# Four moves at the first batches of three stages, and the last batch's schedule a step forward

## The chip, the cores and the metric

The kernel runs on one core of a Trainium2 chip. The metric is the device time of one execution in microseconds. The engines are TensorE (PE in the rows, its weight loads PEld), VectorE (DVE), ScalarE (ACT), GpSimd (POOL) and SyncE (SP, which issues most DMAs).

## The reference, cut to what matters

Four layers, each on x of 8 batches of 256 tokens by 512 features: an attention over the context, an attention over channels, a transformer layer (two attentions over tokens and a gelu MLP), and a recurrent block. In all but the first two the change has a place:

```
# tokens: q, k, v of the normalised rows; then
x = x + gelu(layernorm(x) @ w1 + b1) @ w2 + b2
# recurrent block
xa = ln(x); sx = previous_token(xa) - xa
xxx = tanh((xa + sx * maa_x) @ maa_w1) ...
r, k, v, g = projections of the five mixtures xm
s = k_t v_t + w_t * s;  out_t = r_t (u * k_t v_t + s)      # the scan over tokens
x1 = x + groupnorm(out) * silu(g) @ Wo.T
xc = ln(x1); sx2 = previous_token(xc) - xc
out = x1 + sigmoid((xc + sx2 * fr) @ Wfr.T) * (square(relu((xc + sx2 * fk) @ Wfk.T)) @ Wfv.T)
```

## The kernel before, in words

Five stages follow one another with a barrier between them: `context_attention`, `channel_attention`, `token_attentions`, `token_mlp`, `recurrent_block`. `Ahead` holds the tiles and `AheadSignals` the semaphores that live across a barrier, so that a stage loads rows and weights for the next one. Each stage has one instruction list per engine, and engines meet by semaphores only; all queues are in order. Semaphores of a ring get a credit first, by `open_loop` on SP (line 38), one instruction for each; an engine that waits on such a semaphore also waits for this.

`token_attentions` splits each fp32 operand in a rounded high part (ScalarE) and a low part (VectorE's subtraction), and a projection is three products of parts. Batch 0's projections are the units Q0, Q1, K0, K1, V0, V1 on TensorE (`fill`, lines 1618 and 1620). SP loads the V weights of the first layer in `before` (line 1460), into two tiles of the probabilities; ScalarE's `before` (from line 1813) keeps Q0, Q1, K0, K1, then rounds V (`round_first_values`, line 1755), and VectorE splits it (line 1915).

`token_mlp` runs 8 steps a batch. In step n TensorE does the hidden unit n (24 matmuls, line 2288), now and then the transposes of the next batch's normalised rows (`turn`, line 2275), and the output unit n - 3 (12 matmuls, line 2303). ScalarE evicts a hidden unit with its square (lines 2342, 2345), does the tanh of the one before (`bend`) and rounds it (`round_hidden`, line 2356). VectorE multiplies (line 2471) and finishes the gelu (`gelu`, line 2463), GpSimd multiplies for the cube (line 2257) and takes the low part (line 2226). During batch 0, twelve halves of weights (`HALVES`) are also rounded by ScalarE (`round_half`, line 2334) and split by VectorE (`split_half`, line 2429); `SPLIT_BY` gives how many by which step: 2, 4, 6, 8, 9, 10, 11, 12. They pass through three staging tiles, and SP reloads one when its half is split. `rows_step(b)` says in which step batch b + 1's statistics are taken; normalising follows a step later, and `turn_half` puts its two groups of transposes 2 and 4 steps behind, with VectorE's split one step after each:

```
for k in halves_in(b, n):
    split_half(k)
if b + 1 < BATCH:
    if n == rows_step(b):       statistics(b + 1); moment(b + 1)
    elif n == rows_step(b) + 1: normalise(b + 1)
    elif turn_half(b, n - 1) is not None: split_turned(...)
```

`recurrent_block` pipelines three batches. Batch b's 16 scans (`step`: VectorE's product, line 3420, and scan, line 3423; GpSimd's product, line 2912; TensorE's spread and sum, lines 3050 and 3061) run along with the units of the batch ahead (A: norm, transposes T, difference SX, low-rank XX, mixtures M, K, V, R, G and C) and of the batch behind them, Z: E, Q, N, O, then LS and LN (norm of x1), T, X (difference and mixes), FK, FR, FV. Tables such as `LAST_SCHEDULE` write out by hand which units stand in which of the 16 steps. A unit in a table costs an engine its own part only; each waits on semaphores for the rest. The first batch has a `PROLOGUE` without scans, in which `keep_busy` issues 52 transposes on TensorE whose result nobody reads (the filler), ahead of XX0 (line 2969). `finish` does the last batch's tail after its last scan.

## Time and profile before

| | us |
|---|---|
| median of 3 runs (3635.02 to 3637.12) | 3635.35 |
| the profiled execution | 3639.3 |
| its span, first to last instruction | 3637.5 |
| TensorE busy | 3411.6 (94%) |
| VectorE busy | 2321.6 (64%) |
| GpSimd busy | 2022.3 (56%) |
| ScalarE busy | 1821.5 (50%) |

A row of the order of time has the start, the duration (of the whole group if it has more than one instruction), the engine, the line, the operation, output and inputs, their shapes and the count; in brackets stands how long the engine was idle before it and what released it. `issue` there means that the profile shows no releaser. Times are microseconds from the span's start.

### The profile page before, as it was taken

The numbers are of one execution on the slowest core, as the hardware profiler recorded it, in microseconds if no ns is written. First come the engines' busy times: TensorE is split into PE (matmuls) and PEld (weight loads), VectorE is DVE, ScalarE is ACT, GpSimd is POOL, SyncE is SP. The second block draws the span as 40 slices with busy tenths as digits, with TensorE's granted clock in tenths as the row PEclk, the third lists the DMA queues.
The fourth block names the chain that finished last, engine by engine and source line by source line (L and its number), as shares of the span: only waits on it lengthen the run. The fifth ranks groups of instructions, "written<-read, shape, count | busy, mean of one in ns | idle before, by whom it ended". The sixth has DMA issues, their size and how long they took to land. (4 is left out here: it accounts for less than half of the span.)

```text
span 3637.5 us, 59766 instructions
## 1 busy us (share of the span) xinstructions
PE 3411.6 (94%) x23502; PEld 2613.9 (72%) x23502; DVE 2321.6 (64%) x2874; ACT 1821.5 (50%) x4228; POOL 2022.3 (56%) x1103
## 2 busy tenths in 40 slices
PE   8989999999999999979999999699998899999978
PEld 6878778877887787657887788599985555555544
DVE  2455565566556656748777877665545678877776
ACT  2134664565456546656776776555543334343322
POOL 2235664575557556625665666455544566767753
PEclk9999999999999999989999999899998899999989
DMA  4331111121112111120002111210003000000000
GB/s 133 109 131 47 68 67 56 59 72 62 48 68 72 60 47 47 59 99 24 31 30 82 53 42 49 92 38 24 24 24 126 13 8 11 18 19 18 13 18 12
DMA packets 114302, 188.80 MB, mean 52 GB/s; under 512 B 18416, under 2 KB 36848, under 8 KB 113520
## 3 DMA queue, kind: packets, MB, share of 16 engines
q1 hardware_dynamic: 111856, 180.89, 14.8%
q8 instruction: 183, 3.00, 0.3%
q10 hardware_dynamic: 2176, 4.19, 0.3%
q14 instruction: 87, 0.71, 0.1%
HBM read 159.89 MB, written 25.17 MB: 51 GB/s over the span
## 5 line engine op out<-in xcount | busy, mean ns | idle before, releaser
L1030 POOL TENSOR_TENSOR l_pr<-l_pr,l_inv 128x1024 f32<-128x1024 f32 x256 | 479.7, 1894 | 383.1 <-DVE l_inv L1092 383.1
L900 ACT ACTIVATE l_pr<-l_ps_s,l_top 128x512 f32<-128x512 f32 x512 | 348.0, 689 | 352.7 <-DVE l_top L1088 275.9
L1547 POOL TENSOR_TENSOR tok_pr<-tok_pr,tok_ma 128x1024 f32<-128x1024 f32 x128 | 305.8, 2411 | 268.5 <-DVE tok_pr L1932 268.5
L2912 POOL TENSOR_TENSOR rec_rs<-rec_sE,rec_rT 128x1024 f32<-128x1024 f32 x128 | 316.7, 2474 | 231.6 <-DVE rec_sE L3423 183.3
L1025 POOL TENSOR_TENSOR l_x_lo<-ahead_piece,l_x_hi 128x1024 fp32r<-128x1024 f32 (+1 forms) x97 | 294.0, 3031 | 154.2 <-ACT l_x_hi L884 154.2
L1088 DVE TENSOR_REDUCE l_top<-l_ps_s 128x2 f32<-128x1024 f32 x256 | 304.1, 1218 | 10.5 <-PE l_ps_s L674 10.4
L3423 DVE TENSOR_TENSOR_SCAN rec_sE<-rec_wE,rec_ps_v 128x1024 f32<-128x1024 f32 x128 | 292.7, 2286 | 4.4
L684 PE MATMUL l_ps_t<-l_ident,l_pr 128*128 128x128 f32 x2048 | 275.7, 278 | 10.5 <-POOL l_pr L1030 4.5
L684 PEld LDWEIGHTS l_ps_t<-l_ident,l_pr 128*128 128x128 f32 x2048 | 225.9, 141 | 77.7 <-issue 60.7
L1807 ACT ACTIVATE tok_pr<-tok_pr,tok_shift 128x256 f32<-128x256 f32 x512 | 253.3, 497 | 10.2 <-DVE tok_shift L1940 9.6
L635 PE MATMUL l_ps_b<-l_x_hi,l_w_lo 128*128 128x256 f32 x784 | 226.7, 289 | 0.0
L635 PE MATMUL l_ps_b<-l_x_hi,l_w_hi 128*128 128x256 f32 x784 | 221.2, 282 | 0.0
L635 PE MATMUL l_ps_b<-l_x_lo,l_w_hi 128*128 128x256 f32 x784 | 221.1, 282 | 0.0
L1940 DVE TENSOR_REDUCE tok_shift<-tok_pr 128x4 f32<-128x1024 f32 x128 | 155.6, 1216 | 48.9 <-POOL tok_pr L1547 48.6
L3420 DVE TENSOR_TENSOR rec_ps_v<-rec_ps_v,rec_kT 128x1024 f32<-128x1024 f32 x128 | 156.5, 1223 | 37.7 <-ACT rec_kT L3274 27.6
L1096 DVE COPY l_pT<-l_ps_t 128x512 f32<-128x512 f32 x256 | 174.3, 681 | 2.9 <-PE l_ps_t L684 2.6
L905 ACT ACTIVATE l_pT<-l_ps_t 128x512 f32<-128x512 f32 x256 | 152.3, 595 | 22.9 <-PE l_ps_t L684 22.8
L1932 DVE TENSOR_TENSOR tok_pr<-tok_ps_s,tok_mk 128x1024 f32<-128x1024 f32 x128 | 155.7, 1217 | 7.4 <-PE tok_ps_s L1630 7.4
L1641 PE MATMUL tok_ps_t<-tok_ident,tok_pr 128*128 128x128 f32 x1024 | 139.1, 280 | 17.5 <-DVE tok_pT L1945 11.1
L1116 DVE TENSOR_TENSOR l_o_lo<-l_ps_a,l_o_hi 128x512 fp32r<-128x512 f32 x64 | 44.2, 691 | 170.0 <-ACT l_o_hi L910 170.0
L662 PE MATMUL l_ps_b<-l_wv_lo,l_x_hi 128*128 128x256 f32 x512 | 149.4, 292 | 1.9 <-DVE l_v_later L1102 0.8
L635 PEld LDWEIGHTS l_ps_b<-l_x_hi,l_w_lo 128*128 128x128 f32 x784 | 148.2, 189 | 2.8 <-issue 1.0
(519 smaller groups left out, 9701.0 us busy)
## 6 DMA issues: line engine op xcount, KB each, us to landing
ahead_piece<-x SPq DMA_DIRECT2D x63, 512.0 KB, 3.9
ahead_piece<-in_c SPq DMA_DIRECT2D x63, 512.0 KB, 4.8
ahead_rows<-x SPq DMA_DIRECT2D x22, 512.0 KB, 3.8
ahead_piece<-in_L_w_qk SPq DMA_DIRECT2D x16, 512.0 KB, 6.0
x<-tok_xb SPq DMA_DIRECT2D x16, 512.0 KB, 2.8
l_xt<-in_xT SPq DMA_DIRECT2D x8, 512.0 KB, 6.3
l_ct<-in_cT SPq DMA_DIRECT2D x8, 512.0 KB, 7.2
l_xn<-in_x SPq DMA_DIRECT2D x8, 512.0 KB, 4.7
```

Of the source, the lines that this page charges most:

```text
L635: mm = pe.matmul(bank[:, here], w[:, part, half * SLOTS + s, :], x[b % 2][:, s, here], start=(s == 0 and w is w_lo), stop=(s == SLOTS - 1 ...
L684: mm = pe.transpose(ps_t[h][:, m, :], pr[t][:, h, m * P:(m + 1) * P], ident[:, :])
L900: act.activation(pr[t][:, h, :], ps_s[:, t % 2, h, :], ACT.Exp, bias=top[:, t, h:h + 1], accum_out=mass[:, t, h:h + 1]).then_inc(exped, 1)
L1025: pool.tensor_tensor(x_lo[b % 2][:, which, :], rows, x_hi[b % 2][:, which, :].bitcast(F32), ALU.subtract).then_inc(x_split, 2 if source is ...
L1030: pool.tensor_tensor(pr[t][:, :, :], pr[t][:, :, :], inv[:, t, :].unsqueeze(2).to_broadcast([P, 2, FEAT]), ALU.mult).then_inc(scaled, 1)
L1088: dve.tensor_reduce(top[:, t, :], ps_s[:, t % 2, :, :], AXIS.X, ALU.max, negate=True).then_inc(topped, 1)
L1096: dve.tensor_copy(pT[1][:, :, t * P:(t + 1) * P], ps_t[1][:, :, :]).then_inc(turned_kept[1], 1)
L1547: pool.tensor_tensor(tile, tile, ma[u][:, :, :].rearrange("p t k -> p (t k)").unsqueeze(1).to_broadcast([P, 2, TT * TOK]), ALU.add).then_i ...
L1807: ins = act.activation(tile, tile, ACT.Exp, bias=shift[n % RING][:, i, m:m + 1], accum_out=mass[n // 2 % 2][:, m, n % 2 * 2 + i:n % 2 * 2 ...
L2912: pool.tensor_tensor(rs[j % 2][:, :, :], sE[j % 2][:, :, :], rT[s][:, :, :], ALU.mult).then_inc(rs_made, 1)
L3420: dve.tensor_tensor(ps_v[j % 2][:, :, :], ps_v[j % 2][:, :, :], kT[s][:, :, 0:TOK], ALU.mult).then_inc(kv_made, 1)
L3423: dve.tensor_tensor_scan(sE[j % 2][:, :, :].rearrange("p c t -> p (c t)"), wE[s][:, :, :].rearrange("p c t -> p (c t)"), ps_v[j % 2][:, :, ...
```

## The change

It has five places.

- `token_attentions`: the two loads of the first V weights stand at the head of SP's list, ahead of the credits; ScalarE rounds them after Q1 is kept, ahead of K0.
- `token_mlp`: `rows_step(0)` returns 2, not 1; ScalarE's `round_hidden` stands ahead of `round_half` in a step; SP loads the recurrent block's columns and first edge after the last half. (The staging tiles get a name for their number; it stays 3.)
- `recurrent_block`, first batch: columns and edge are there already; `maa_w1` is loaded ahead of the credits; the edge is copied ahead of T0; VectorE, not GpSimd, takes the difference, in two halves behind T0 and T1; the filler has 30 transposes; the first states are loaded later in SP's list.
- `FIRST_TENSOR_SCHEDULE`: G0 ahead of C in step 1.
- `LAST_SCHEDULE`: LN joins LS in step 8, and all Z units behind it stand one step earlier; VectorE's X too.

```diff
@@ -63,6 +63,9 @@
     def __init__(self, nc, rows_ctx, ctx):
...
+        self.cols = rows_ctx.enter_context(nc.sbuf_tensor("ahead_cols", [P, 16, FT], F32))
+        self.edge = rows_ctx.enter_context(nc.sbuf_tensor("ahead_edge", [P, FT, 2], F32))
         self.rows = rows_ctx.enter_context(nc.sbuf_tensor("ahead_rows", [P, TT, FEAT], F32))
@@ -1413,6 +1416,9 @@
         def _(sp):
+            for k in range(2):
+                source = layers[0].w["QKVO".index("V")][2 * k * P:2 * (k + 1) * P, :].rearrange("(t p) n -> p t n", p=P)
+                sp.dma_start(first_v(k), source).then_inc(first_v_loaded, 16)
             open_loop(sp, loop_sems)
@@ -1455,9 +1461,6 @@
                     sp.dma_start(qk_sb[i][:, :, :], layers[i].qk).then_inc(small_loaded, 16)
-                for k in range(2):
-                    source = layers[0].w["QKVO".index("V")][2 * k * P:2 * (k + 1) * P, :].rearrange("(t p) n -> p t n", p=P)
-                    sp.dma_start(first_v(k), source).then_inc(first_v_loaded, 16)
                 load_x(1, 1, 0)
@@ -1823,9 +1826,11 @@
                 act.wait_ge(bias_scaled, len(layers))
-                for unit in UNITS[:4]:
+                for unit in UNITS[:2]:
                     keep(1, 0, unit, 0)
                 round_first_values()
+                for unit in UNITS[2:4]:
+                    keep(1, 0, unit, 0)
                 normalise(1, 1)
@@ -2090,7 +2096,7 @@
-        return 1 if b == 0 else 0
+        return 2 if b == 0 else 0
@@ -2207,6 +2213,9 @@
                 load_half(k)
+            next_cols, next_state = recurrent
+            sp.dma_start(ahead.cols[:, :, :], next_cols).then_inc(following.piece_loaded[0], 16)
+            sp.dma_start(ahead.edge[:, :, :], next_state[0:1, :, :, :].rearrange("o p t n -> p (o t) n")[:, :, 0:2]).then_inc(following.piece_loaded[1], 16)
             sp.wait_ge(here.last_stored, 16)
@@ -2375,10 +2384,10 @@
                     bend(*before(b, n, 1))
+                if b or n:
+                    round_hidden(*before(b, n, 1))
                 for k in halves_in(b, n):
                     round_half(k)
-                if b or n:
-                    round_hidden(*before(b, n, 1))
                 if turn_half(b, n) is not None:
@@ -2513,7 +2522,7 @@
     FIRST_TENSOR_SCHEDULE = (
-        "L:R1 A:T0 A:T1", "L:C L:G0", "A:XX0 A:XX1", "L:G1", "A:Mwk0", "A:Mwk1", "A:Mvr0 A:Mvr1", "A:D1", "A:K0",
+        "L:R1 A:T0 A:T1", "L:G0 L:C", "A:XX0 A:XX1", "L:G1", "A:Mwk0", "A:Mwk1", "A:Mvr0 A:Mvr1", "A:D1", "A:K0",
         "A:K1 A:Mgd0", "A:R0 A:Mgd1", "A:R1", "A:V0", "A:V1 A:C B:T0 B:T1", "A:G0 B:XX0 B:XX1", "A:G1 B:Mwk0 B:Mwk1")
@@ -2540,10 +2549,10 @@
     LAST_SCHEDULE = (
-        "", "Z:E", "Z:Q Z:I", "Z:N1", "Z:N2", "Z:N3", "Z:O0", "Z:O1", "Z:LS", "Z:LN", "Z:T0 Z:T1 Z:X", "Z:XA Z:XR",
-        "Z:FK0", "Z:FK1", "Z:FR0", "Z:FR1")
+        "", "Z:E", "Z:Q Z:I", "Z:N1", "Z:N2", "Z:N3", "Z:O0", "Z:O1", "Z:LS Z:LN", "Z:T0 Z:T1 Z:X", "Z:XA Z:XR", "Z:FK0",
+        "Z:FK1", "Z:FR0", "Z:FR1", "")
     LAST_VECTOR_SCHEDULE = (
-        "", "Z:E", "", "Z:I", "", "Z:N3", "", "", "Z:LS", "", "", "Z:X", "", "", "", "")
+        "", "Z:E", "", "Z:I", "", "Z:N3", "", "", "Z:LS", "", "Z:X", "", "", "", "", "")
     SUB, HALF = 4, P // 2
@@ -2626,8 +2634,8 @@
         w_loaded, ident_made, const_made, power_made = sem("w_loaded"), sem("ident_made"), sem("const_made"), sem("power_made")
-        a_edge_loaded = sem("a_edge_loaded")
-        cols_loaded, x_loaded, st_loaded, z_loaded, stored = sem("cols_loaded"), here.rows_loaded, [sem(f"st_loaded{u}") for u in range(2)], sem("z_loaded"), sem("stored", 16)
+        a_edge_loaded, halves_shifted = here.piece_loaded[1], sem("halves_shifted")
+        cols_loaded, x_loaded, st_loaded, z_loaded, stored = here.piece_loaded[0], here.rows_loaded, [sem(f"st_loaded{u}") for u in range(2)], sem("z_loaded"), sem("stored", 16)
         a_filled, z_filled, z_kept = sem("a_filled", NA), sem("z_filled", NZ), sem("z_kept", NZ)
@@ -2759,6 +2767,7 @@
         def _(sp):
+            sp.dma_start(m1[:, :, :], maa_w1.rearrange("(t p) n -> p t n", p=P)).then_inc(m1_loaded, 16)
             open_loop(sp, loop_sems)
@@ -2784,16 +2793,13 @@
-            sp.dma_start(col[:, :, :], cols).then_inc(cols_loaded, 16)
-            load_edge(0)
-            sp.dma_start(m1[:, :, :], maa_w1.rearrange("(t p) n -> p t n", p=P)).then_inc(m1_loaded, 16)
-            load_st(0, 0)
             sp.dma_start(m2[:, :, :], maa_w2).then_inc(w_loaded, 16)
...
             sp.dma_start(mean_of[:, :], group_mean).then_inc(w_loaded, 16)
+            load_st(0, 0)
             for n in "kvrg":
@@ -2859,6 +2865,8 @@
                                        ALU.add).then_inc(mixtures, 1)
+                elif unit == "SX" and b == 0:
+                    pool.wait_ge(mixed_x, of(b, 1, 0))
                 elif unit == "SX":
@@ -2966,7 +2974,7 @@
                 if unit == "XX0" and b == 0:
-                    keep_busy(pe, ps_acc[:, 0, 0:P], ident, 52)
+                    keep_busy(pe, ps_acc[:, 0, 0:P], ident, 30)
                     pe.wait_ge(const_made, CONSTANTS)
@@ -3166,7 +3174,7 @@
                     act.wait_ge(mixtures, of(b - 1, 5, 4))
-                elif unit == "T1":
+                if unit == ("T1" if b else "T0"):
                     act.wait_ge(a_edge_loaded, (b + 1) * 16)
@@ -3335,8 +3343,14 @@
                         dve.wait_ge(cols_loaded, 16)
-                    dve.wait_ge(shifted, of(b, 1, 0))
+                    else:
+                        dve.wait_ge(shifted, of(b, 1, 0))
                     for c in range(FT):
+                        if b == 0 and c % 2 == 0:
+                            dve.wait_ge(keeps(b, f"T{c // 2}"), kept_by(b, f"T{c // 2}"))
+                            dve.tensor_tensor(sx[:, c:c + 2, :], xaT[:, c:c + 2, 0:TOK], xaT[:, c:c + 2, 1:TOK + 1],
+                                              ALU.subtract).then_inc(halves_shifted, 1)
+                            dve.wait_ge(halves_shifted, c // 2 + 1)
                         ins = dve.scalar_tensor_tensor(out=xm[0][:, c, :], in0=sx[:, c, :], scalar=col[:, MAA_X, c:c + 1],
```

## Rows read from the trace of the kernel before

**Rows 1.** By stage: window, busy of each engine (instructions), granted clock, DMA share, GB/s
```profile
1588.00:2334.00 746.00, 699.00 (x6562) 571.25 (x6562) 552.23 (x688) 498.50 (x1427) 424.23 (x255) 0.97 0.15 50
2334.00:2723.00 389.00, 373.56 (x2400) 337.56 (x2400) 210.80 (x230) 203.43 (x430) 204.79 (x156) 0.98 0.12 40
2723.00:3637.00 914.00, 799.65 (x3918) 500.40 (x3918) 667.57 (x581) 304.78 (x689) 558.30 (x304) 0.95 0.08 26
```

**Rows 2.** Order of time at the token attentions: start, duration, instruction, idle before it
```profile
1592.37 0.34 SPq L1456 DMA_DIRECT2D tok_ln_cols<-in_L_ln  x1
...
1596.90 1.91 ACT L1772 ACTIVATE tok_lnT<-tok_ps_t,tok_ln_cols 128x256 f32<-128x256 f32 x4
...
1606.21 0.84 ACT L1747 ACTIVATE tok_qT<-tok_ps_s,tok_qk_cols 128x256 f32<-128x256 f32 x2 [1.84 <-PE tok_ps_s L1620]
...
1611.17 0.63 PE L1620 MATMUL tok_ps_s<-tok_lnT_lo,tok_w_hiK 128*128 128x256 f32 x4
...
1612.57 2.00 ACT L1755 ACTIVATE tok_w_hiV<-tok_pr 128x1024 fp32r<-128x1024 f32 x2
...
1617.06 2.05 PE L1618 MATMUL tok_ps_p<-tok_w_hiV,tok_lnT_hi 128*128 128x512 f32 x4 [5.26 <-issue]
...
1624.47 1.09 PE L1618 MATMUL tok_ps_o<-tok_w_hiV,tok_lnT_lo 128*128 128x512 f32 x4
...
1625.40 1.04 PE L1590 MATMUL tok_ps_t<-tok_ident,ahead_xn 128*128 128x128 f32 x8
```

**Rows 3.** DMAs, 1588 to 1612: count, KB each, median us from issue to landing
```profile
tok_pr<-in_L_xattn_w_qkv SPq DMA_DIRECT2D x2, 512.0 KB, 4.1
...
tok_qk_cols<-in_L_qk SPq DMA_DIRECT2D x2, 4.0 KB, 2.0
```

**Rows 4.** Order of time in the MLP's first batch
```profile
2353.72 1.06 ACT L2334 ACTIVATE mlp_w_hi<-mlp_xb 128x1024 fp32r<-128x1024 f32 x1 [2.52 <-DMA mlp_xb<-in_L_xattn_w]
...
2363.78 1.09 PE L2275 MATMUL mlp_ps_t<-mlp_ident,ahead_xn 128*128 128x128 f32 x4 [10.98 <-DVE ahead_xn L2408]
...
2371.26 0.40 PE L2303 MATMUL mlp_ps_y<-mlp_w_lo,mlp_hid_hi 128*128 128x512 f32 x1
...
2373.59 1.83 DVE L2463 SCALAR_TENSOR_TENSOR ahead_piece<-ahead_piece 128x512 f32<-128x512 f32 x1
...
2383.16 2.41 POOL L2238 TENSOR_TENSOR mlp_xb<-ahead_rows,mlp_b 128x1024 f32<-128x1024 f32 x1
...
2384.65 1.21 DVE L2471 TENSOR_SCALAR ahead_piece<-ahead_piece 128x512 f32<-128x512 f32 x1 [2.61 <-ACT ahead_piece L2345]
...
2391.26 0.28 PE L2288 MATMUL mlp_ps_h<-mlp_ln_hi,mlp_w_lo 128*128 128x256 f32 x1
```

**Rows 5.** Order of time at the recurrent block's start
```profile
2725.05 7.51 PE L59 MATMUL rec_ps_acc<-rec_ident 128*128 128x128 f32 x52
...
2727.51 1.02 ACT L3184 ACTIVATE rec_xaT<-rec_ps_a,rec_cols 128x256 f32<-128x256 f32 x2 [11.55 <-DMA rec_cols<-in_L_cols]
...
2731.83 1.68 DVE L3340 SCALAR_TENSOR_TENSOR rec_xm<-rec_sx,rec_cols,rec_xaT 128x256 f32<-128x256 f32 x4 [7.34 <-POOL rec_sx L2865]
...
2733.65 2.51 PE L2988 MATMUL rec_ps_a<-rec_xm,rec_m 128*128 128x256 f32 x10 [1.10 <-DVE rec_xm L3340]
```

**Rows 6.** Order of time around unit C of batch 0
```profile
2787.95 1.08 PE L2998 MATMUL rec_ps_a<-rec_sx,rec_hs_u 128*32 128x256 f32 x8 [3.48 <-issue]
...
2789.82 5.63 PE L2936 MATMUL rec_ps_a<-rec_xm,rec_w_g 128*128 128x256 f32 x16
...
2792.06 1.67 DVE L3340 SCALAR_TENSOR_TENSOR rec_xm<-rec_sx,rec_cols,rec_xaT 128x256 f32<-128x256 f32 x4 [1.75 <-POOL rec_sx L2865]
```

**Rows 7.** Order of time in the last batch
```profile
3563.11 5.65 DVE L3403 SCALAR_TENSOR_TENSOR rec_xk<-rec_sq,rec_cols,rec_xcT 128x256 f32<-128x256 f32 x4 [0.88 <-POOL rec_sq L2888]
...
3579.84 1.23 DVE L3420 TENSOR_TENSOR rec_ps_v<-rec_ps_v,rec_kT 128x1024 f32<-128x1024 f32 x1 [0.73 <-ACT rec_kT L3274]
...
3589.74 0.69 DVE L3432 TENSOR_TENSOR rec_bonus<-rec_ps_acc,rec_bonus 128x512 f32<-128x512 f32 x1 [6.34 <-PE rec_ps_acc L3061]
```

More of the change, by code:

```diff
@@ L2070, in weight_columns, with token_mlp @@
     return w1[:, i * FEAT:(i + 1) * FEAT].rearrange("(t p) n -> p t n", p=P)
-def token_mlp(nc, semaphores, x, w1_d, w2_d, ln_cols, b1, b2, out, ahead, here, following):
+def token_mlp(nc, semaphores, x, w1_d, w2_d, ln_cols, b1, b2, out, ahead, here, following, recurrent):
     HID = 4 * FEAT
@@ L2080, in token_mlp @@
     HALVES = [(n, i, k) for n, i in (("w2", 0), ("w1", 2), ("w2", 1), ("w1", 3), ("w2", 2), ("w2", 3)) for k in range(2)]
-    LAST_IN_XB = (len(HALVES) - 1) // 3 * 3
+    STAGES = 3
+    LAST_IN_XB = (len(HALVES) - 1) // STAGES * STAGES
     SPLIT_BY = (2, 4, 6, 8, 9, 10, 11, 12)
@@ L2126, in token_mlp @@
         xb = sb("xb", [P, TT, FEAT])[:, :, :]
-        spare = sb("spare", [P, 2, FEAT])
+        spare = [sb(f"spare{i}", [P, 2, FEAT])[:, :, :] for i in range(1)]
         w2_lo = sb("w2_lo", [P, 2 * CHUNKS, FEAT], F32R)
         res = sb("res", [P, TT, FEAT])[:, :, :]
-        stages = (xb, res, spare[:, :, :])
+        stages = (xb, res, *spare)
         ps_h = [ps(f"ps_h{i}", [P, 2, TOK]) for i in range(2)]
@@ L2140, in token_mlp @@
             sem(n) for n in ("norm_loaded", "b1_loaded", "b2_loaded", "ident_made", "const_made"))
-        half_loaded = [sem(f"half_loaded{i}") for i in range(3)]
+        half_loaded = [sem(f"half_loaded{i}") for i in range(STAGES)]
         piece_hi, piece_split, half_hi, half_split = (sem(n) for n in ("piece_hi", "piece_split", "half_hi", "half_split"))
@@ L2193, in load_half @@
                 n, i, half = HALVES[k]
-                if k >= 3:
-                    sp.wait_ge(half_split, k - 2)
+                if k >= STAGES:
+                    sp.wait_ge(half_split, k - STAGES + 1)
                 if n == "w1":
@@ L2199, in load_half @@
                     source = w2_d[(4 * i + 2 * half) * P:(4 * i + 2 * half + 2) * P, :]
-                sp.dma_start(stages[k % 3], source.rearrange("(t p) n -> p t n", p=P)).then_inc(half_loaded[k % 3], 16)
+                sp.dma_start(stages[k % STAGES], source.rearrange("(t p) n -> p t n", p=P)).then_inc(half_loaded[k % STAGES], 16)
             sp.dma_start(ln_sb[:, :, :], ln_cols).then_inc(norm_loaded, 16)
@@ L2332, in round_half @@
             def round_half(k):
-                act.wait_ge(half_loaded[k % 3], 16 * (k // 3 + 1))
-                act.activation(half_of(k, 0), stages[k % 3], ACT.Copy).then_inc(half_hi, 1)
+                act.wait_ge(half_loaded[k % STAGES], 16 * (k // STAGES + 1))
+                act.activation(half_of(k, 0), stages[k % STAGES], ACT.Copy).then_inc(half_hi, 1)
             def evict(b, n):
@@ L2428, in split_half @@
                     dve.wait_ge(here.last_stored, 16)
-                dve.tensor_tensor(half_of(k, 1), stages[k % 3], half_of(k, 0).bitcast(F32), ALU.subtract).then_inc(half_split, 1)
+                dve.tensor_tensor(half_of(k, 1), stages[k % STAGES], half_of(k, 0).bitcast(F32), ALU.subtract).then_inc(half_split, 1)
             def next_statistics():
@@ L2575, in recurrent_block @@
         mean_of = sb("mean_of", [P, P])
-        NC = 16
-        col = sb("cols", [P, NC, FT])
+        col = ahead.cols
         LN1_W, LN1_B, LN2_W, LN2_B, MAA_X, DECAY0, U, GN_W, GN_B, FFN_K, FFN_R, STACK = range(12)
@@ L2586, in recurrent_block @@
         st = [sb(f"st{u}", [P, FT, 2 + GROUP]) for u in range(2)]
-        edge, a_edge = sb("edge", [P, FT, 2]), sb("a_edge", [P, FT, 2])
+        edge, a_edge = sb("edge", [P, FT, 2]), ahead.edge
         xaT, sx = sb("xaT", [P, FT, TOK + 1]), sb("sx", [P, FT, TOK])
@@ L2638, in recurrent_block @@
         shifted, mixed_x, products, mixtures, decayed, g_bent, v_hi_kept = (
-            sem("shifted", 1), sem("mixed_x", 1), sem("products", 5), sem("mixtures", 5), sem("decayed", 1), sem("g_bent", 2), sem("v_hi_kept", 2))
+            sem("shifted", 1, 3), sem("mixed_x", 1), sem("products", 5), sem("mixtures", 5), sem("decayed", 1), sem("g_bent", 2), sem("v_hi_kept", 2))
         spread_v, kv_made, seeded, scanned, rs_made, summed = (
@@ L3530, in build @@
     semaphores.clear(kept)
-    token_mlp(nc, semaphores, x4, ap["L2_xattn_w1"], ap["L2_xattn_w2"], ap["L2_ln3"], ap["L2_b1"], ap["L2_b2"], x5, ahead, for_mlp, for_recurrent)
+    token_mlp(nc, semaphores, x4, ap["L2_xattn_w1"], ap["L2_xattn_w2"], ap["L2_ln3"], ap["L2_b1"], ap["L2_b2"], x5, ahead, for_mlp, for_recurrent,
+              (ap["L3_cols"], ap["L3_state"]))
     early.close()
```

## The prediction

> **What bounds the kernel now.** I read the table of stages first: TensorE is busy for 94% of the token attentions, 96% of the MLP and 87% of the recurrent block [rows 1], so an edit pays only where TensorE stands still, and all edits of this change lie at such places: the first batch of three stages, and the last batch of the last one. Then I read the order of time at each place. In the token attentions TensorE ends the K projections at 1611.8 and starts V at 1617.06 [rows 2]. In the MLP it stands 10.98 us before the transposes of batch 1, because VectorE has not normalised those rows [rows 4]. At the recurrent block's start ScalarE waits for the column constants until 2727.51, and a filler of 52 transposes bridges the time until 2733.65 [rows 5]. In the last batch VectorE needs 5.65 us for four small mixes and at the end waits 6.34 us for the last sum [rows 7].
>
> **1. First V weights (token attentions).** Two edits belong together: SP issues the two V loads ahead of its credits, and ScalarE rounds V behind the second Q unit, not behind the second K unit. Now TensorE's last K matmul ends at 1611.8 (1611.17 + 0.63), ScalarE first keeps that unit, rounds V from 1612.57 for 2.00, VectorE's split takes about 2.4, and TensorE idles 5.26 [rows 2]. After: ScalarE is free at 1607.05 (1606.21 + 0.84), rounds until 1609.1, still ahead of the K0 unit's end at about 1609.0, and VectorE, idle there, has split by 1611.5. TensorE is through K1 at 1611.8 and goes straight on: 5.3 us off the path. The 24 V matmuls took 8.34 us (1617.06 to 1625.40), the first four 2.05, the last four 1.09; with groups of four 0.93 apart, as the last two are (1624.47 to 1625.40), all would take 5.6: the idle had dropped the granted clock to 1.2 GHz. Without it another 2.7 goes. Next late would be the normalised rows of batch 1 (ScalarE 1612.7 to 1614.2) and the mask; both are early. Sum: -8.1. The next short stall, at 1627.5 to 1629.6, stays.
> The loads cost SP two issues of 0.45 us ahead of its credits and ahead of the small loads. The small ones land 2.0 us after issue now [rows 3]; SP issues the first of four at 1592.37 [rows 2], the last 1.4 later, so it would be 1594.7, landed at 1596.7, and ScalarE wants it at 1596.90 [rows 2]: cost 0, up to 0.5 if it lands late. The Trainium skill ("DMA: Bandwidth & Descriptors", Queues, rings and completion order) says that each ring consumes descriptors in order, so the small loads would now queue behind 1 MB of V; an estimate from the 4.1 us to landing puts V's end at 1595, before their own 1596.7, and the sum is the same by either.
>
> **2. The MLP's first batch.** Two edits: rows_step(0) goes from 1 to 2, so that statistics, normalise, transposes and split of batch 1 come a step later (transposes in steps 4 and 6, splits in 5 and 7); and ScalarE rounds the hidden layer (round_hidden) ahead of the weight halves. I wrote out the order of each engine, step by step, with the durations of the rows: a hidden unit 2.7, an output unit 2.8 (TensorE does 7 units and one transpose group from 2371.26 to 2391.26 [rows 4]), eviction 1.43, a rounded half 0.95, a split 1.2, gelu 0.6, GpSimd's products 1.3, a load 4. Two things matter in it. A VectorE operation that meets a GpSimd one waits until that ends: 1.83 for a gelu of 0.68, 1.21 for a multiply of 0.43, while GpSimd's bias addition ran until 2385.57 [rows 4]. And evict 2 stands behind a rounded half whose load lands at 2353.72 [rows 4], in both orders. For the kernel before this schedule gives the transposes at 2363.9 (row: 2363.78) and batch 1's first hidden unit at 2390.2 (row: 2391.26), so I trust it to about 1 us.
> For the changed kernel: output unit 0 is no longer behind the transposes and runs at 2353.8, hidden 4 at 2356.6 to 2359.5. Then TensorE comes to the transposes, in step 4. Their rows are normalised in VectorE's step 3, behind two more halves: gelu 1 ends 2358.4, round_hidden 1 2359.0, halves 4 and 5 are rounded by 2361.0 and split by 2362.7, statistics 2364.1, gelu 2 2365.1, halves 6 and 7 rounded by 2367.7 and split by 2370.35, normalised 2371.3. TensorE waits 11.8, not 10.98, and starts output 1 at 2371.7, now at 2371.26 [rows 4]: **the first wait is moved, not removed**. From there the later splits bite. Batch 1's hidden unit needs the second split of its rows, now in step 7. ScalarE evicts hidden 7 by 2393.0, gelu 6 ends 2395.5 (behind GpSimd's product), round_hidden 6 2396.1, half 11, which the new order puts behind it, 2397.1, its split 2398.6, cast and split of the rows 2399.7. TensorE would be ready at 2391.7: a **new wait of 8 us**. From there the stage has no slack: its TensorE is idle 15.4 us in all [rows 1], mostly the known wait. So 2399.7 less 2391.3 is +8.4; the slow clock behind the first long wait costs 1.2 as it does now (the schedule has full clock, and this is carried into the second chain), and behind the second wait 1.2 more: +10.8. Bounds: +6 if the waits for GpSimd vanish, +13 if both waits cost 2.7 in clock, as in part 1.
> The rows show VectorE's operation blocked for the whole of GpSimd's. The Trainium skill ("SBUF — State Buffer", SBUF: two separate sides) gives that as an exclusive lock of a shared port pair, which speaks against packing gelu and splits between GpSimd's products: schedule against schedule the change loses 9.5 with it (2390.2 to 2399.7) and 5.9 without it. By that rule, the trace agrees.
>
> **3. The recurrent block's start.** Columns and edge are loaded during the MLP, m1 ahead of the credits, the difference of batch 0 moves from GpSimd (1.89) to VectorE in halves, between ScalarE's two evictions, and the filler has 30 transposes. TensorE's transposes start some 0.45 later, since SP's credits stand behind m1's issue. ScalarE evicts at once (2725.3 to 2727.2, now 2727.51 to 2729.66), VectorE subtracts (0.69 twice) and mixes (1.68): done 2729.5, now 2733.51. The filler now needs 7.51 [rows 5]; at the full clock, that the second half of it has, one costs about 0.12 (eight in 1.04 with the last one's drain [rows 2]), so 22 fewer save 2.6 by the clock and 3.2 by the mean. It ends at 2730.7: **-3.0** against 2733.65, and the filler, not the mix, is late last. Bounds -2.5 and -4. The two added DMAs in the MLP hide behind SP's wait for the biased rows; the six narrow weights have 1.9 us left, the wide ones 4.
>
> **4. G0 ahead of C.** TensorE waits 3.48 for GpSimd's product before C [rows 6]. G0 fills that hole, but batch 1's XX0 then waits for its mix (2792.06 + 1.67), so that the hole comes back and the slow clock with it: -0.5, between -2 and +1.
>
> **5. Last batch.** From LN on, each unit of the batch in front comes a step earlier. VectorE's mix X (5.65 of which 4 are waiting for GpSimd [rows 7]) then comes before scan 11 instead of behind it: step 12 starts at 3569.6 to 3570.8 for 3568.68. ScalarE's seed of scan 15 falls behind FR0's tanh, as it falls behind FK1 now (0.73 wait [rows 7]), and scan 15 ends 2 to 3 us later. In return GpSimd has no square in front of the last two products and TensorE no FR1 before the last sum. The last sum comes at 3589.8 by the schedule, for 3590.1 now: -0.3, between -2 and +2.
>
> **Sum.** -8.1 + 10.8 - 3.0 - 0.5 - 0.3 = -1.1. The profiled execution took 3639.3 (span 3637.5 and 1.8 around it), 4.0 above the median of 3635.35. So 3638.2 there and **3634.3** as a median. The measurement can tell about 0.2%, 7.3 us, from no change.
>
> **Rivals.** (a) The MLP's edits cost nearly nothing: the second split is ready when TensorE asks for it, since VectorE and ScalarE are ahead after the long first wait. For: at step 4 they have evicted hidden 4 already. Against: the chain of step 7 holds six dependent operations. MLP +0.7, total -11.2: 3624.2. Chance 0.22. (b) The forecast, 0.66, own range 3629 to 3640. (c) Slower: in the MLP every one of seven steps loses its race against GpSimd's product, 1.3 us each on the chain, 9.1 on top: MLP +19.9, total +8.0, 3643.4. It decides from an MLP loss of 19. Against: the schedule has most races lost already. Chance 0.06. (d) The V rounding does not come in time, because its load lands late; then -8.1 falls away and the total is +7.0: 3642.4. Against: V lands 12 us before its new reader. Chance 0.02. (e) The gains of parts 1 and 3 alone with an even larger effect on the clock: 3619, chance 0.04.
> Faster by over 0.2% (under 3628.1): (a), (e) and a little of (b), 0.28; slower (over 3642.6): 0.06; within: 0.66. Range 3622 to 3641.
>
> **What would show it.** Part 1: V's first matmul follows K1 without idle and the granted clock stays 1.00 there. Part 2: in the MLP a wait of about 12 us before the transposes, behind five hidden units and one output unit, and one of about 8 before batch 1's first hidden unit; if the second is absent, (a) holds. Part 3: XX0 at 7.4 us from the stage's start instead of 10.3. Part 5: the last sum within 2 us. The stage lengths then differ by -8, +11, -4. I am wrong if the MLP's stage grows by under 6.

## The result, and the profile after

The changed kernel takes **3646.8 us** (median of 7 runs, 3642.1 to 3647.9) beside 3635.0 of the kernel before on the same chip: ratio 1.0031, interval 1.0021 to 1.0041. It is slower by 11.8 us. A later series on another chip gave 3648.7 beside 3634.0, 1.0038 (1.0024 to 1.0051). The forecast was 3634.3 with a range to 3641. In the run mlp_undone below, one of ten executions took 4249.5 at a clock of 0.745; it counts in the median that is given there and not in the ratio.

The profiled execution has a span of 3644.4. Its table of stages, with the columns of [rows 1]:

```profile
1587.90:2326.20 738.30, 693.93 (x6562) 567.93 (x6562) 552.04 (x687) 499.50 (x1428) 424.20 (x256) 0.98 0.15 50
2326.20:2726.50 400.30, 376.15 (x2400) 339.14 (x2400) 207.32 (x230) 203.64 (x430) 199.37 (x156) 0.97 0.11 38
2726.50:3644.40 917.90, 793.85 (x3896) 495.34 (x3896) 668.97 (x583) 305.15 (x689) 556.32 (x303) 0.95 0.08 26
```

From one stage's first instruction on GpSimd to the next one's, before and after: token attentions 744.6 and 738.2, MLP 388.5 and 400.4, recurrent block 914.1 and 917.9. The forecast said -8.1, +10.8 and -3.8; it is -6.4, +11.9 and +3.8, and the unchanged stages ahead differ by -2.4.

**Token attentions**, order of time, to be read beside [rows 2]. V follows K without idle, but the small loads land late:

```profile
1587.91 1.71 SPq L1421 DMA_DIRECT2D tok_pr<-in_L_xattn_w_qkv  x2
...
1591.73 0.34 SPq L1462 DMA_DIRECT2D tok_ln_cols<-in_L_ln  x1
...
1595.95 1.93 ACT L1775 ACTIVATE tok_lnT<-tok_ps_t,tok_ln_cols 128x256 f32<-128x256 f32 x4 [0.88 <-DMA tok_qk_cols<-in_L_qk]
...
1607.13 2.00 ACT L1758 ACTIVATE tok_w_hiV<-tok_pr 128x1024 fp32r<-128x1024 f32 x2
...
1611.89 1.09 PE L1621 MATMUL tok_ps_p<-tok_w_hiV,tok_lnT_hi 128*128 128x512 f32 x4
...
1617.48 1.03 PE L1593 MATMUL tok_ps_t<-tok_ident,ahead_xn 128*128 128x128 f32 x8
```

V runs from 1611.89 to 1617.48, 5.6 us instead of 8.3, at a granted clock of 1.00. But ScalarE starts on the transposes 8.0 us from the stage's start, not 6.6 (1596.90 less 1590.33), and all projections start 1.5 later. The view of DMAs gives the small loads' way from issue to landing [rows 3]:

```profile
tok_qk_cols<-in_L_qk SPq DMA_DIRECT2D x2, 4.0 KB, 2.9
```

**The MLP**: what TensorE waits for, of the kernel before and then of the changed one (engine, line, releaser: us in total, times, longest).

```profile
PE mlp_ps_t L2275 <- DVE ahead_xn L2408: 11.0, 1, 11.0
PE mlp_ps_t L2275 <- POOL mlp_ident L51: 3.0, 1, 3.0
PE mlp_ps_y L2303 <- POOL mlp_hid_lo L2226: 0.5, 1, 0.5
```

```profile
PE mlp_ps_t L2284 <- DVE ahead_xn L2417: 10.6, 1, 10.6
PE mlp_ps_h L2297 <- DVE mlp_ln_lo L2426: 8.5, 2, 7.3
PE mlp_ps_t L2284 <- POOL mlp_ident L51: 3.0, 1, 3.0
PE mlp_ps_y L2312 <- POOL mlp_hid_lo L2235: 1.7, 2, 1.2
```

The old wait is still there and one of 7.3 has joined it: batch 1's first hidden unit waits for the second split of its rows. The chain in front of it, in order of time, GpSimd's product, VectorE and then TensorE:

```profile
2385.71 1.26 POOL L2266 TENSOR_TENSOR ahead_piece<-ahead_piece 128x512 f32<-128x512 f32 x1 [2.11 <-DVE ahead_piece L2480]
2385.72 1.80 DVE L2472 SCALAR_TENSOR_TENSOR ahead_piece<-ahead_piece 128x512 f32<-128x512 f32 x1
...
2389.16 1.45 DVE L2438 TENSOR_TENSOR mlp_w_lo<-mlp_spare,mlp_w_hi 128x1024 fp32r<-128x1024 f32 x1 [1.64 <-ACT mlp_w_hi L2343]
...
2390.53 0.41 DVE L2424 CAST mlp_ln_hi<-mlp_ln_raw 128x512 fp32r<-128x512 f32 x1
2390.97 0.69 DVE L2426 TENSOR_TENSOR mlp_ln_lo<-mlp_ln_raw,mlp_ln_hi 128x512 fp32r<-128x512 f32 x1
...
2391.72 0.58 PE L2297 MATMUL mlp_ps_h<-mlp_ln_hi,mlp_w_lo 128*128 128x256 f32 x1 [7.34 <-DVE mlp_ln_lo L2426]
```

It is the chain of the forecast (`gelu` is line 2472 here, `split_half` 2438, the rows' cast and split 2424 and 2426): the gelu blocked by GpSimd's product (1.80 for 0.68), 1.64 of waiting for the rounded half 11, its split, the rows' cast and split.

**Recurrent block, the start** [rows 5]:

```profile
2728.34 1.93 ACT L3192 ACTIVATE rec_xaT<-rec_ps_a,ahead_cols 128x256 f32<-128x256 f32 x4
2728.69 4.99 PE L59 MATMUL rec_ps_acc<-rec_ident 128*128 128x128 f32 x30
...
2733.52 2.66 PE L2996 MATMUL rec_ps_a<-rec_xm,rec_m 128*128 128x256 f32 x11
```

XX0 starts 7.0 us from the stage's start, 10.2 before. **And behind it**, around C of batch 0 [rows 6]:

```profile
2788.07 0.61 PE L3006 MATMUL rec_ps_a<-rec_sx,rec_hs_u 128*32 128x256 f32 x8
...
2791.79 1.67 DVE L3354 SCALAR_TENSOR_TENSOR rec_xm<-rec_sx,ahead_cols,rec_xaT 128x256 f32<-128x256 f32 x4 [1.81 <-POOL rec_sx L2873]
...
2796.84 0.66 DVE L3392 SCALAR_TENSOR_TENSOR rec_g<-rec_g,rec_ps_a 128x512 f32<-128x512 f32 x1
...
2797.56 3.78 PE L2996 MATMUL rec_ps_a<-rec_xm,rec_m 128*128 128x256 f32 x8 [8.20 <-DVE rec_g L3392]
```

The mix for batch 1's XX0 is ready at 2793.5, but TensorE waits until 2797.56 for VectorE to keep G0, which stands behind scan 2. **The last batch** [rows 7]:

```profile
3567.89 5.65 DVE L3417 SCALAR_TENSOR_TENSOR rec_xk<-rec_sq,ahead_cols,rec_xcT 128x256 f32<-128x256 f32 x4 [2.77 <-POOL rec_sq L2896]
...
3585.20 1.23 DVE L3434 TENSOR_TENSOR rec_ps_v<-rec_ps_v,rec_kT 128x1024 f32<-128x1024 f32 x1 [1.12 <-ACT rec_kT L3282]
3586.47 2.29 DVE L3437 TENSOR_TENSOR_SCAN rec_sE<-rec_wE,rec_ps_v 128x1024 f32<-128x1024 f32 x1
3589.86 1.23 DVE L3434 TENSOR_TENSOR rec_ps_v<-rec_ps_v,rec_kT 128x1024 f32<-128x1024 f32 x1 [1.11 <-ACT rec_kT L3282]
...
3596.61 0.69 DVE L3446 TENSOR_TENSOR rec_bonus<-rec_ps_acc,rec_bonus 128x512 f32<-128x512 f32 x1 [3.20 <-PE rec_ps_acc L3069]
```

The mix X stands for 2.77 + 5.65 us in front of scan 11, and the products of scans 14 and 15 wait 1.1 each for seeds. VectorE's last wait is 3.2 instead of 6.3, but the last addition comes 870.1 us into the stage, 866.3 before.

### The profile page after: what moved, and what is told of

It is laid out like the page before. It is cut to its first block and busy times, and to the rows that moved or that the text cites. A ratio compares the mean times of both kernels' runs of the same rounds, so it can differ in the third digit from the quotient of the medians.

```text
span 3644.4 us, 59722 instructions
## 1 busy us (share of the span) xinstructions
PE 3401.5 (93%) x23480; PEld 2606.6 (72%) x23480; DVE 2321.0 (64%) x2876; ACT 1823.8 (50%) x4228; POOL 2015.0 (55%) x1102
## 5 line engine op out<-in xcount | busy, mean ns | idle before, releaser
L1810 ACT ACTIVATE tok_pr<-tok_pr,tok_shift 128x256 f32<-128x256 f32 x512 | 253.4, 497 | 10.8 <-DVE tok_shift L1945 10.2
L2266 POOL TENSOR_TENSOR ahead_piece<-ahead_piece 128x512 f32<-128x512 f32 x64 | 87.3, 1364 | 121.8 <-DVE ahead_piece L2480 121.8
L2297 PE MATMUL mlp_ps_h<-mlp_ln_hi,mlp_w_lo 128*128 128x256 f32 x512 | 144.0, 281 | 8.5 <-DVE mlp_ln_lo L2426 8.5
```

What stands on the lines that cost most here:

```text
L1810: ins = act.activation(tile, tile, ACT.Exp, bias=shift[n % RING][:, i, m:m + 1], accum_out=mass[n // 2 % 2][:, m, n % 2 * 2 + i:n % 2 * 2 ...
```

## The experiments

Fifteen runs followed, each a whole kernel; two of them repeat the kernel before and the changed one. A name in -undone is the changed kernel with one part taken back. Each table row gives the median, its ratio to the kernel before on the same chip with the interval, and the three stages of the profiled execution.

| kernel | us | ratio (interval) | token | MLP | recurrent |
|---|---|---|---|---|---|
| before | 3635.0 | 1 | 744.6 | 388.5 | 914.1 |
| before, second profile | 3634.4 | 1.0004 (0.9994 to 1.0014) | 740.5 | 388.9 | 911.5 |
| changed | 3646.8 | 1.0031 (1.0021 to 1.0041) | 738.2 | 400.4 | 917.9 |
| changed, second profile | 3648.7 | 1.0038 (1.0024 to 1.0051) | 735.3 | 401.1 | 918.2 |
| mlp_undone | 3635.4 | 1.0002 (0.9993 to 1.0012) | 739.0 | 389.1 | 916.5 |
| step_undone | 3634.5 | 1.0000 (0.9990 to 1.0009) | 737.7 | 391.5 | 915.3 |
| order_undone | 3639.2 | 1.0011 (1.0001 to 1.0020) | 736.5 | 397.0 | 914.2 |
| v_loads_late | 3643.5 | 1.0023 (1.0013 to 1.0032) | 736.4 | 400.4 | 917.8 |
| tok_undone | 3650.4 | 1.0042 (1.0027 to 1.0057) | 737.1 | 401.3 | 918.0 |
| swap_undone | 3638.4 | 1.0011 (1.0002 to 1.0020) | 731.9 | 401.5 | 911.3 |
| last_undone | 3640.7 | 1.0018 (1.0009 to 1.0028) | 731.6 | 401.3 | 917.2 |
| g0_kept_early | 3637.3 | 1.0010 (1.0000 to 1.0020) | 736.5 | 400.7 | 907.6 |
| rows_first | 3633.4 | 0.9999 (0.9989 to 1.0010) | 731.7 | 392.3 | 916.8 |
| gains_only | 3625.4 | 0.9977 (0.9968 to 0.9986) | 730.2 | 390.0 | 911.8 |
| gains_and_g0 | 3625.3 | 0.9978 (0.9969 to 0.9987) | 735.5 | 389.7 | 911.7 |
| token_only | 3625.5 | 0.9976 (0.9966 to 0.9986) | 736.4 | 389.2 | 911.2 |
| turn_later | 3617.4 | 0.9956 (0.9943 to 0.9970) | 731.6 | 383.5 | 911.6 |

**How far one kernel's stages differ.** The kernel before once more (before_again), no edit:

> The kernel before, unchanged, for a second profile: how far do the stages of one kernel differ from execution to execution? Expected: the last two stages within 0.5 us of 388.5 and 914.1, the token attentions within 3 of 744.6 (the unchanged first stages differed by 3 between kernels). Rival: the stages of the same kernel differ by as much as the parts that are to be told apart, 5 us or more.

The MLP is within 0.4, the recurrent block 2.6 apart, which is more than the 0.5 expected, and the token attentions 4.1. So the MLP's column can be read to about a microsecond; a single entry of the other two says little, and there I compare the starts of single instructions, or means of several kernels.

### The MLP

mlp_undone takes both edits back in the changed kernel, step_undone and order_undone one each:

```
-        return 2 if b == 0 else 0        # mlp_undone, step_undone
+        return 1 if b == 0 else 0
-                if b or n:               # mlp_undone, order_undone
-                    round_hidden(*before(b, n, 1))
                 for k in halves_in(b, n):
                     round_half(k)
+                if b or n:
+                    round_hidden(*before(b, n, 1))
```

> The changed kernel with both MLP edits taken back (statistics of batch 1 in step 1, the weight halves rounded ahead of the hidden layer); all else stays changed. My theory: the MLP's 400.3 us fall back to 388.5 +- 1, with one long wait on TensorE before the transposes (about 11 us) and none before batch 1's first hidden unit; the total falls by 11.8, to about 3635. Rival (the stage is longer because it starts otherwise, or because SP loads the recurrent block's columns in it): the stage stays at 398 to 400 and the total near 3646.

> The changed kernel with the statistics of batch 1 back in step 1, but the hidden layer still rounded ahead of the halves. My theory (the later rows cost most, since their second split becomes the last thing that batch 1's first hidden unit needs): MLP stage 390 us (388.5 and 1.5 by the order written out by hand), total about 3636.5. Rival (the order of rounding is what delays the halves and with them all splits): MLP 396 to 400, total 3643 to 3647.

> The changed kernel with statistics in step 2 kept, but the halves rounded ahead of the hidden layer again. My theory: the two waits stay, the second about 5.5 us before batch 1's first hidden unit: MLP stage 395.5 to 398, total 3641 to 3644. Rival (only both edits together lose): MLP within 1.5 of 388.5, total near 3635.

The stage is 389.1, 391.5 and 397.0, each where my theory put it (step_undone 1.5 above the 390 named, nearer to it than to the rival). The medians of step_undone and order_undone, 3634.5 and 3639.2, are about 2 below what I expected. The later rows alone cost about 8, the order alone 2.5, both 11.9. What TensorE waits for in order_undone:

```profile
PE mlp_ps_h L2297 <- DVE mlp_ln_lo L2426: 5.7, 2, 4.5
PE mlp_ps_t L2284 <- DVE ahead_xn L2417: 5.5, 1, 5.5
PE mlp_ps_y L2312 <- POOL mlp_hid_lo L2235: 4.7, 2, 4.2
```

The wait before the transposes looks halved, 5.5 for 10.6, but one of 4.2 now stands ahead of output 0. The transposes, in the changed kernel and in order_undone:

```profile
2361.29 1.09 PE L2284 MATMUL mlp_ps_t<-mlp_ident,ahead_xn 128*128 128x128 f32 x4 [10.57 <-DVE ahead_xn L2417]
```

```profile
2362.68 1.09 PE L2284 MATMUL mlp_ps_t<-mlp_ident,ahead_xn 128*128 128x128 f32 x4 [5.53 <-DVE ahead_xn L2417]
```

Both start 35.1 us into their stage, as soon as VectorE has normalised the rows. So the order of rounding does not move those rows here; it only decides whether TensorE waits all at once or partly ahead of output 0. What the new order costs comes behind, in the second wait: 7.3 instead of 4.5. (With the rows in step 1 the order does move them: step_undone's transposes start 1.4 later than mlp_undone's.)

rows_first splits the turned rows ahead of multiply, gelu and halves:

```
             for b, n in order(1):
...
+                if b == 0 and turn_half(b, n - 1) is not None:
+                    split_turned(b + 1, turn_half(b, n - 1))
                 if b < BATCH:
                     dve.wait_ge(squared, of(b, CHUNKS, n))
...
-                    elif turn_half(b, n - 1) is not None:
+                    elif b and turn_half(b, n - 1) is not None:
```

> The changed kernel, but in the MLP's first batch VectorE splits the turned rows of batch 1 at the head of steps 5 and 7, ahead of the gelu and of the weight halves. If the wait of 7.3 us before batch 1's first hidden unit is the chain in front of the second split (multiply, gelu behind GpSimd, half 11), it falls below 1.5 us and the MLP takes 393 to 396 us instead of 400.4. Rival (the wait stands for TensorE's own late transposes, which come as late as before): the wait stays above 5 and the MLP at 398 to 401.

```profile
PE mlp_ps_t L2284 <- DVE ahead_xn L2417: 11.7, 1, 11.7
PE mlp_ps_t L2284 <- POOL mlp_ident L51: 3.0, 1, 3.0
PE mlp_ps_y L2312 <- POOL mlp_hid_lo L2235: 1.4, 2, 0.9
PE mlp_ps_h L2297 <- DVE mlp_ln_lo L2426: 0.6, 1, 0.6
```

The second wait is gone (0.6) and the stage falls by 8.1 to 392.3, 0.7 under the range expected: the chain in front of that split is the cause of two thirds of the loss. The slow clock behind the wait went too: from batch 1's first hidden unit to its next transposes, the same code, it is 16.7 us at a granted clock of 0.83 in the changed kernel and 14.0 at 1.00 in rows_first. The first wait stays at 11.7.

### The recurrent block

swap_undone writes C ahead of G0 again, g0_kept_early leaves G0 ahead but keeps it earlier:

```
     FIRST_TENSOR_SCHEDULE = (                               # swap_undone
-        "L:R1 A:T0 A:T1", "L:G0 L:C", "A:XX0 A:XX1",
+        "L:R1 A:T0 A:T1", "L:C L:G0", "A:XX0 A:XX1",
...
     FIRST_VECTOR_SCHEDULE = (                               # g0_kept_early
-        "", "L:C A:SX", "L:G0", "", "L:G1",
+        "", "L:C L:G0 A:SX", "", "", "L:G1",
```

> The changed kernel with C ahead of G0 again in the first batch's step 1. My theory: XX0 of batch 1 shares its half of PSUM with whatever unit stands two places ahead; behind C it waits only for its mix, behind G0 it waits until VectorE has kept G0, which stands behind scan 2. With C in front the wait of 8.2 us before XX0 falls to about 2, the scans from 4 on come 4 to 5 us earlier at first, of which 1.6 was caught up again in the changed kernel too: total 3 us less than the changed kernel, about 3643.5. Rival (the hole only moves, and the wait before XX0 is for its mix): scan 4 within 1 us of the changed kernel's.

> The changed kernel, G0 still ahead of C, but VectorE keeps G0 in step 1, between C and the mix of batch 1, not in step 2 behind scan 2. If XX0 waits 8.2 us because G0's half of PSUM is kept so late, that wait now ends with the mix or the early keep: scan 4 comes 4 to 5 us earlier in relation to the stage's start than in the changed kernel (80.2), at 75.5 to 76, and the recurrent stage takes 911 to 913 instead of 918. Rival (TensorE's order of G0 and C itself delays C and with it the mix): scan 4 stays at 79 to 80.

I took the start of every scan from the order of time of each kernel, from the stage's start on, and subtracted that of the kernel before (first column):

```
batch, step     before  changed  swap_un.  g0_early  last_un.  gains  before_again
0, 3             75.53    -3.4     -3.3      -9.8      -3.3     -2.4     -2.2
0, 4             78.98    +1.2     -3.3      -8.9      +1.3     -2.4     -2.2
0, 15           149.97    +0.1     -3.5      -9.2      +0.3     -2.3     -2.5
7, 0            784.67    +1.9     -3.5      -7.6      +2.7     -2.3     -2.5
7, 11           836.52   +11.7     +5.5      +1.7      +3.1     -2.3     -2.5
7, 12           846.51    +5.1     -1.1      -4.9      +3.1     -2.3     -2.5
7, 15           857.69    +6.9     +0.4      -3.4      +3.1     -2.3     -2.5
last addition   866.32    +3.8     -2.8      -6.5      +3.1     -2.3     -2.5
```

Between scans 3 and 4 of batch 0 the changed kernel loses 4.6; with C in front nothing; with G0 kept early 0.9. Part of it is caught up: by scan 15 of batch 0 the nine profiles with this order and the late keep have lost 3.5 to 3.7 since scan 3, swap_undone nothing. In g0_kept_early XX0 waits for its mix:

```profile
2788.44 3.75 PE L2996 MATMUL rec_ps_a<-rec_xm,rec_m 128*128 128x256 f32 x8 [4.24 <-DVE rec_xm L3354]
```

So the cause is shown: the kernel gives its units two PSUM tiles in turn, in the order of the units (`bank_of`, line 2735; the expectations call each tile a half of PSUM), and with G0 ahead of C the unit XX0 gets the tile that G0 leaves, which VectorE keeps only behind scan 2. Both kernels gained more than I expected. g0_kept_early's stage is 907.6 for 911 to 913, but of its lead over the changed kernel at scan 4, 10.1, there were 6.4 at scan 3 already, nearly all from an earlier start of that execution and not from the edit. swap_undone's stage is 6.6 shorter and its median 8.4 lower, where I had 3.

last_undone puts back the two tables of the last batch (the change's last hunk of tables, reversed):

> The changed kernel with the last batch's two tables as before. My theory: the last batch, from its first scan to the last addition, becomes 1.75 us shorter (the seeds of scans 14 and 15 are no longer behind the evictions of FK1 and FR0, and scan 11 is not behind the mix X); total about 3644.5, hard to tell from the changed kernel. Rival (the whole difference of 1.75 comes from the clock and from how the batch starts): last batch unchanged within 0.5.

From the last batch's first scan to the last addition last_undone takes 0.4 longer than the kernel before, the changed kernel 1.9 and swap_undone, with the changed last batch, 0.8. With the step forward it is 0.8 to 1.9 in all kernels, without it 0 to 0.4, and the mix X is where the scans lose it: +8.4 between scans 10 and 11, of which 6.5 come back at scan 12, in whose way X stood before. The median fell by 6.1, more than the last batch can give. The token stage of that profile is 6.6 shorter with the same code, so I don't read the median as the price of the tables.

### The token attentions

v_loads_late puts the two loads behind the small ones, tok_undone takes the rounding back as well, token_only is the kernel before with the one edit of ScalarE:

```
                     sp.dma_start(qk_sb[i][:, :, :], layers[i].qk).then_inc(small_loaded, 16)
+                for k in range(2):                                   # v_loads_late
+                    source = layers[0].w["QKVO".index("V")][2 * k * P:2 * (k + 1) * P, :].rearrange("(t p) n -> p t n", p=P)
+                    sp.dma_start(first_v(k), source).then_inc(first_v_loaded, 16)
-                for unit in UNITS[:4]:                               # token_only
+                for unit in UNITS[:2]:
                     keep(1, 0, unit, 0)
                 round_first_values()
+                for unit in UNITS[2:4]:
+                    keep(1, 0, unit, 0)
```

> The changed kernel with the two V loads back behind the small loads; V is still rounded ahead of K0. My theory: the loads in front put the credits and the small loads 1.5 us later and cost 1.5 at the first Q unit, while V is early enough in either place: the token stage falls from 738.3 to 736.8 or a little less, and V still follows K without idle time. Rival (the loads had to be in front for V to be there in time): a wait on the V weights appears at their rounding and the stage is as long as before the change, 743 to 745.

> The changed kernel with both edits of the token attentions taken back. My theory: their stage is 744.6 us again (738.3 with the edits), with 5.3 us idle before V: total 3652 to 3653. Rival (the 6.3 are given back by a later wait that follows the earlier one, so that the stage's gain shows only in this stage's own window and not in the total): total within 2 of the changed kernel.

With the loads late, ScalarE starts on the transposes at 6.58 us of the stage and TensorE on the projections at 9.72, with the loads in front at 8.03 and 11.19; V is rounded without waiting in both. The 1.5 us are shown at their place, and 1.1 more goes in the Q projections, which take 7.1 at a granted clock of 0.79 with the loads in front and 6.0 at 1.00 without. V's last matmul is followed by the transposes of the next rows, in v_loads_late:

```profile
1609.45 1.10 PE L1621 MATMUL tok_ps_p<-tok_w_hiV,tok_lnT_hi 128*128 128x512 f32 x4
...
1615.07 1.04 PE L1593 MATMUL tok_ps_t<-tok_ident,ahead_xn 128*128 128x128 f32 x8
```

That is 26.9 us into the stage, 29.6 in the changed kernel and 35.1 in the kernel before. Over all profiles it is 26.9 (four times) and 28.4 with V rounded early and the loads late, 28.5 to 30.3 with the loads in front (nine), and 33.8 to 35.2 with neither edit (three): as means 27.2, 29.8 and 34.7. So rounding early gains 7.5 at its place and the loads in front give back 2.6. The stage's length blurs this: 730.2 to 736.4 with the loads late, 731.6 to 739.0 with the loads in front, and tok_undone, where the idle 5.26 before V is back and V ends 5.6 later, has 737.1, which is 1.1 shorter than the changed kernel and not the 744.6 expected. Its median rose by 3.6, not by 6.

### Together

gains_only is the kernel before with the rounding ahead of K0 (loads late) and the recurrent start; gains_and_g0 adds G0 ahead of C with its early keep.

> The kernel before with the parts that gained alone: V rounded ahead of K0 (its loads behind the small ones as before), and the recurrent block's start. MLP, the order of C and G0 and the last batch as before. My theory: token attentions -7.8, recurrent start -3.3, nothing else: 3624 to 3626, 11 less than before. Rival (the recurrent start is given back within the first batch, because each batch's scans wait for something with its own pace): 3627 to 3629.

> The parts that gained (V rounded ahead of K0 with its loads behind the small ones, the recurrent start), and G0 ahead of C with its early keep. MLP and last batch as before. If the early keep frees XX0, G0 fills TensorE's hole ahead of C and the recurrent stage takes 1 to 3 us less than the 911.8 of the gains alone: 3623 to 3625. Rival (C and the mix come later by G0's 3.7 us of matmuls and nothing is gained): 911.8 to 914, 3625 to 3628.

> The kernel before with one edit: ScalarE rounds V ahead of K0. If the token attentions carry the whole gain of the kernel with the gains alone (3625.4, 9.2 less than before) and the recurrent start is given back to the clock, 3625 to 3627. Rival (the start's 2 to 3 us reach the end): 3627.5 to 3629.

All three take 3625.3 to 3625.5, 9 less than before. G0 in front with its early keep brings 0.6 at scan 3 and nothing at scan 15, so my 1 to 3 us for gains_and_g0 did not come. token_only bears on part 3: without any edit of the recurrent start it is as fast, within intervals of 3.6 us either way. The start is real at XX0 (6.9 to 8.2 us against 10.2 in both profiles of the kernel before) and absent at scan 0: 54.7 with the gains alone, 54.2 in token_only, 54.9 and 57.1 in the two profiles of the kernel before. What lies between follows the clock: in the first 10 us of the stage TensorE had 0.67 in gains_only and 1.00 in token_only, and 0.86 and 1.00 from 40 to 55. The same code of the stage, 10 to 25 us into it, in the changed kernel and in order_undone (granted clock third from the end):

```profile
2736.52:2751.52 15.00, 10.23 (x44) 5.89 (x42) 6.05 (x12) 3.74 (x9) 8.02 (x3) 0.69 1.03 389
```

```profile
2734.52:2749.52 15.00, 10.16 (x58) 6.85 (x57) 6.82 (x12) 4.96 (x14) 9.10 (x4) 1.00 1.03 384
```

At 0.69, a mean over stretches at 1.2 and at 2.4 GHz, TensorE gets through 44 matmuls, at 1.00 through 58, and scan 0 starts 3.6 us apart (53.6 and 50.0).

after_again is the changed kernel, no edit. turn_later adds to gains_only, in the MLP, the splits of rows_first and this:

```
-        return {2: 0, 4: 1}.get(n - rows_step(b)) if b + 1 < BATCH else None
+        return ({3: 0, 5: 1} if b == 0 else {2: 0, 4: 1}).get(n - rows_step(b)) if b + 1 < BATCH else None
```

> The changed kernel once more, for a second profile and for its median beside the others. If the earlier difference of 11.8 us to the kernel before holds on another chip: 3643 to 3647, MLP 400 to 401.5, from the last batch's first scan to its last addition 83.4 us (81.65 before the change). Rival (the earlier runs were at the upper edge by chance): 3639 to 3642.

> The gains alone, and in the MLP's first batch TensorE's transposes a step later, VectorE's two splits of those rows at the head of steps 5 and 7; statistics and normalising stay in steps 1 and 2, and the halves are rounded first, as before the change. If the first long wait is there because normalising comes late, and output 0 and hidden 4 (5.5 us) can be done in it, the wait falls from 11 to 5 or 6 us and no second one comes: MLP 383 to 386 instead of 389 to 390, total 3620 to 3622. Rival (the hidden layer or a staged half is what comes late next, so that the wait goes to output 0 or hidden 4): MLP 388 to 391, total 3625.

The second run of the changed kernel came out 2 above what I expected (3648.7 for 3643 to 3647), its MLP at 401.1. TensorE's waits in turn_later's MLP:

```profile
PE mlp_ps_y L2312 <- POOL mlp_hid_lo L2235: 4.5, 2, 4.0
PE mlp_ps_t L2284 <- POOL mlp_ident L51: 3.0, 1, 3.0
```

The wait of 11 us is gone; one of 4.0 before output 0 is left. MLP 383.5, total 3617.4: **16.6 us less than the kernel before**, ratio 0.9956, and 2.6 less than the lower end expected. What the change's MLP edits aimed at was to be had, by moving the transposes without the normalising and putting the splits first; against gains_only it is 8.0 in the medians and about 6 in the stage. No run has the later transposes without the earlier splits.

## Why the prediction was wrong

**The MLP (part 2)** was right, in size (+11.9 for +10.8) and in mechanism: first wait 10.6 for 11.8, second 7.3 for 8, the same chain of operations, and rows_first removes the second. At batch 1's first hidden unit the stage is 9.3 later, where I had 9.6; the clock behind the second wait then cost 2.6, where I had 1.2. That the first wait is moved and not removed holds for the later step alone too: the rows are ready no earlier.

**Token V (part 1)**: V without idle and at full clock is as predicted, and with the loads late the rounding gains 7.5 for 8.1. The step that failed is "cost 0, up to 0.5" for the loads in front. I had counted two issues of 0.45; the two took 1.71 on SP, so the first small load was issued 3.8 us into the stage instead of 2.0 (1591.73 and, in [rows 2], 1592.37), and they took 2.9 us to land instead of 2.0 [rows 3]. Together 2.7; before, the last one landed 1.2 ahead of its reader, so ScalarE was late by 1.5, and with the slower clock behind it the start of V by 2.7 against v_loads_late. The Trainium skill ("DMA: Bandwidth & Descriptors", Queues, rings and completion order) says that each ring consumes descriptors in order, which speaks for the longer landing behind 1 MB of V. By that rule, the trace agrees as far as it goes: V landed 5.9 and 7.3 us into the stage, and the four small loads, issued from 3.8 on, at 6.8 to 8.0, two of them ahead of V's second load. I had let my own estimate cancel it. As a mean of the kernels with the loads in front the stage takes 735.4, of the three without the edits 740.7: 5 us, not 8.

**The recurrent start (part 3)**: -3.0 at XX0 came as -3.2. The step that failed is the unspoken one, that XX0's lead reaches the first scan. No run shows that it does: scan 0 starts at 54.2 in token_only and at 54.6 to 54.7 in the three kernels that add the start to it (two of them with another edit beside it), whose stages take 911.6 to 911.8 for token_only's 911.2. With an edit of the MLP's waits beside it, as in the changed kernel, scan 0 comes at 47.9 to 53.8, and no run has that without the start, so there a part may arrive. Why the clock takes the lead back is not shown.

**G0 ahead of C (part 4)** is the largest error: -0.5, bounds to +1, measured +4.6 at scan 4, 3.6 at the end of batch 0 and 5.4 at the last batch's start (the changed kernel against swap_undone, +1.9 and -3.5). The step that failed is "XX0 then waits for its mix": it waited 8.2 for VectorE to keep G0. I had looked at what XX0 reads and not at what its PSUM tile still holds. Of the 5.4, about 1.9 is one jump at scan 15 of batch 6, in unchanged code; it stands in the changed kernel's first profile and in five others. There eight matmuls of FR (line 2951), behind a wait of 2.7, take 5.4 us with a granted clock of 0.72 around them; in swap_undone, behind a wait of 1.2, they take 3.7 at 1.00. What sets off the longer wait is not shown.

**The last batch (part 5)**: -0.3 between -2 and +2, measured +1.9, or 0.8 to 0.9 in three kernels without that jump (mlp_undone, step_undone, swap_undone). The step that failed is the price of the mix in front: X before scan 11 delayed step 12 by 2.5 to 3.2 (I had 0.9 to 2.1), since VectorE also waits 2.8 in front of it. With the seeds behind FK1 and FR0, 1.1 of waiting each, scan 15 came 3.9 to 5.1 later where I had 2 to 3, and the last wait gave back 3.1 of it (3.2 for 6.3), as I had it.

**Sum.** -5 + 12 + 4.5 is +11.5, with 4.5 as the recurrent block with all its edits (a mean of 916.8 in eight profiles, 914.2 to 918.2) less that without any (912.3 in three); the medians say +11.8 and +14.7. The result lies 12.5 us above the forecast: by these means about 8 of it in the recurrent block, where I had -3.8, 3 in the token attentions and 1 in the MLP. Rivals (c) and (d), the two on the slower side, looked for it in the MLP and in V's loads. I had no rival for a unit that waits for a buffer.
